# A fused adaLN, attention and mixture-of-experts kernel: the loop over batches written out, and two of eight probability tiles of a head pair normalised by VectorE

## What is computed

```python
h = _layernorm(x, axis=-1) * (1 + ca) + sa
qkv = x @ qkv_w.T                       # x is h here; B, S = 4, 512
scores = jnp.einsum('bhqd,bhkd->bhqk', q, k) * scale + bias
attn = jax.nn.softmax(scores, axis=-1)
a = jnp.einsum('bhqk,bhkd->bhqd', attn, v)
x = x + ga * (a.transpose(0, 2, 1, 3).reshape(B, S, 1024) @ o_w.T)
h = _layernorm(x, axis=-1) * (1 + cb) + sb      # and on to the experts
```

## Time and profile before

| | us |
|---|---|
| median of 3 runs | 1016.47 (1014.36 to 1022.89) |
| the profiled execution, whole time | 1013.81 |
| its span in the profile | 1012.0 |
| PE busy, whole span | 953.2 (94%) |
| DVE busy | 769.4 (76%) |
| ACT busy | 679.4 (67%) |
| POOL busy | 398.1 (39%) |

### The profile page before, as it was taken

How to read it: one execution, slowest core, us unless ns; L and a number is a source line. 1 busy time by engine, 2 the same in 40 slices (tenths; PEclk the granted TensorE clock), 3 DMA queues, 4 the chain that set the end, 5 groups by cost and what they waited for, 6 DMA issues and landing times.

```text
span 1012.0 us, 16804 instructions
## 1 busy us (share of the span) xinstructions
PE 953.2 (94%) x4592; PEld 690.6 (68%) x4592; DVE 769.4 (76%) x1452; ACT 679.4 (67%) x1168; POOL 398.1 (39%) x260
## 2 busy tenths in 40 slices
PE   4889999899998999999969699999999999999997
PEld 2546666566665666666524578888888888888886
DVE  5757667566665666766647589999999999999997
ACT  3556666466665666666626477877777777777775
POOL 0578888688886888888910000000000000000000
PEclk9999999899999999999979899999999999999999
DMA  7885445256444445534200899999999999999991
GB/s 205 258 234 119 97 119 126 63 124 142 113 96 101 96 118 125 125 90 99 66 19 27 204 221 219 223 222 222 223 222 222 221 224 221 223 220 225 220 206 41
DMA packets 71096, 160.39 MB, mean 158 GB/s; under 512 B 10273, under 2 KB 36193, under 8 KB 60945
## 3 DMA queue, kind: packets, MB, share of 16 engines
q1 hardware_dynamic: 71056, 159.97, 70.1%
HBM read 105.60 MB, written 2.42 MB: 107 GB/s over the span
## 4 chain that ended last, share of the span: by engine, by line
PE 84%; DMA 4%; DVE 4%; issue 3%; ACT 2%; SPq 1%; POOL 1%; POOLq 0%; DVEq 0%; ACTq 0%
PE ps L620 40%; PE ps L433 11%; PE ps L420 10%; PE ps L409 5%; PE ps L411 5%; PE ps L383 4%; PE ps L446 3%; PE ps L394 2%; DMA strips<-in_L_ffn_w_down 2%; DMA k_low<-qk 1%; POOL prob L859 1%; DMA comb_rows<-strips 1%; PE ps L538 1%; PE ps L540 0%; DVE qk L959 0%
## 5 line engine op out<-in xcount | busy, mean ns | idle before, releaser
L859 POOL TENSOR_SCALAR prob<-prob,rinv 128x512 f32<-128x512 f32 x256 | 397.9, 1567 | 111.3 <-DVE rinv L993 109.1
L706 ACT ACTIVATE prob<-prob,nmax 128x512 f32<-128x512 f32 x256 | 182.9, 716 | 150.9 <-DVE nmax L976 150.8
L620 PE MATMUL ps<-hT,wT 128*128 128x512 f32 x960 | 244.2, 390 | 0.3 <-DVE wT L1145 0.3
L1164 DVE TENSOR_TENSOR PT<-v_sb,strips 128x1024 f32<-128x1024 f32 x160 | 196.0, 1225 | 41.4 <-ACT v_sb L830 28.3
L830 ACT ACTIVATE v_sb<-ps 128x1024 f32<-128x1024 f32 x160 | 164.5, 1028 | 77.9 <-PE ps L620 77.4
L620 PEld LDWEIGHTS ps<-hT,wT 128*128 128x128 f32 x960 | 180.8, 189 | 39.0 <-ACT strips L805 1.1
L620 PE MATMUL ps<-stack,wT 128*128 128x512 f32 x640 | 198.1, 391 | 9.2 <-DVE wT L1151 9.2
L204 DVE COPY PT<-ps 128x512 f32<-128x512 f32 x128 | 88.4, 691 | 141.2 <-PE ps L420 138.7
L1151 DVE TENSOR_TENSOR wT<-PT,stack 128x1024 fp32r<-128x1024 f32 x160 | 195.0, 1219 | 0.0
L976 DVE CUSTOM_DVE_ANT_0 prob<-ps,strips 128x512 f32<-128x512 f32 x256 | 165.0, 681 | 11.5 <-issue 8.0
L822 ACT CAST stack<-PT 128x1024 fp32r<-128x1024 f32 x160 | 166.6, 1041 | 8.8 <-DVE PT L1164 8.8
(11 more groups left out here) (105 smaller groups left out, 731.1 us busy)
## 6 DMA issues: line engine op xcount, KB each, us to landing
strips<-comb_rows SPq DMA_DIRECT2D x158, 512.0 KB, 10.9
stack<-qk SPq DMA_DIRECT2D x128, 256.0 KB, 3.8
k_low<-qk SPq DMA_DIRECT2D x64, 128.0 KB, 3.9
hT<-qk SPq DMA_DIRECT2D x64, 128.0 KB, 3.8
strips<-bias_rows SPq DMA_DIRECT2D x3, 1792.0 KB, 13.9
strips<-in_L_ffn_w_gate SPq DMA_DIRECT2D x80, 64.0 KB, 9.8
strips<-in_L_ffn_w_down SPq DMA_DIRECT2D x80, 64.0 KB, 11.0
strips<-bias_rows SPq DMA_DIRECT2D x2, 896.0 KB, 5.4
```

The lines of the kernel that those rows point to most:

```text
L620: last = nc.tensor.matmul(ps[:, bank + c, :], weights(a), rows(m, c), start=start and k == 0, stop=stop and k == 2, skip_group_check=True)
L706: nc.scalar.activation(prob[:, u, :], prob[:, u, :], ACT.Exp, bias=nmax[:, u:u + 1], scale=-1.0, accum_out=rsum[:, u:u + 1]).then_inc(s_ex ...
L859: nc.gpsimd.tensor_scalar(prob[:, u, :], prob[:, u, :], rinv[:, u:u + 1], None, ALU.mult).then_inc(s_prob, 1)
L1164: nc.vector.tensor_tensor(weighted[:, k % 4, :], silu[:, k % 2, :], cb[:, r, half * HALF:(half + 1) * HALF], ALU.mult).then_inc(s_mul, 1)
```

## The change

Three things change, all in attention.

First, the loops over batches are written out: `Fori` becomes a Python `for` on PE, ACT, DVE, SP and POOL, and all semaphore targets become constants. Second, of each pair's eight tiles, units 3 and 7 are normalised by DVE, right behind the reciprocal of their two units, and the other six by POOL; a second semaphore, `normalised_by_dve`, counts DVE's. Third, the order of DVE's work within a segment changes: `invert_sums` moves ahead of the copies, and `update_x` and `new_statistics` move from the end of a batch's last pair (n = 9) into the first segment of the next one (n = 2 of the next batch).

```diff
--- before.py
+++ after.py
@@ -165,7 +165,8 @@
         s_s, s_ttr, s_exp, s_t = sem("scores"), sem("biased"), sem("exped"), sem("transposed")
         s_ca, s_cd = sem("copied_by_act"), sem("copied_by_dve")
         s_v, s_vc, s_pv = sem("v_projected"), sem("v_copied"), sem("pv_done")
-        s_rinv, s_prob, s_o = sem("sums_inverted"), sem("normalised"), sem("o_copied")
+        s_rinv, s_o = sem("sums_inverted"), sem("o_copied")
+        s_prob, s_prob_dve = sem("normalised_by_pool"), sem("normalised_by_dve")
         s_ymm, s_yg, s_ytr, s_x2 = sem("y_added"), sem("y_gated"), sem("y_transposed"), sem("x_updated")
 
 
@@ -196,6 +197,12 @@
         def copied(b, g):
 
             return (s_ca if g % 2 == 0 else s_cd), b * (G // 2) + (g // 2 + 1)
+
+        def normalised(b, g):
+
+            if g % 4 == 3:
+                return s_prob_dve, b * (G // 4) + g // 4 + 1
+            return s_prob, b * (G // 4 * 3) + (g // 4 * 3 + g % 4 + 1)
 
         def copy_unit(copy, n, u):
 
@@ -289,7 +296,7 @@
             sp.dma_start(wdsT[:, :], down_shared_t).then_inc(ld["small"], 16)
             sp.dma_start(ebias[:, 0:1], expert_bias[0:P, :]).then_inc(ld["small"], 16)
             sp.dma_start(ebias[0:E - P, 1:2], expert_bias[P:E, :]).then_inc(ld["small"], 16)
-            with sp.Fori(0, B - 1) as b:
+            for b in range(B - 1):
                 for n in range(2, HPAIRS + 2):
                     if n == HPAIRS - 2:
                         sp.wait_ge(s_v, b * HPAIRS + HPAIRS)
@@ -413,7 +420,7 @@
 
             def transpose_probs(b, n, u):
                 g = UNITS * n + u
-                pe.wait_ge(s_prob, b * G + (g + 1))
+                pe.wait_ge(*normalised(b, g))
                 if g >= 2:
                     pe.wait_ge(*copied(b, g - 2))
                 for kb in range(QT):
@@ -506,7 +513,7 @@
             pair(0, 1)
             pe.wait_ge(w_split, 6)
             pe.wait_ge(ld["ow"], 16)
-            with pe.Fori(0, B - 1) as b:
+            for b in range(B - 1):
                 for n in range(2, HPAIRS + 2):
                     pair(b, n)
             for n in range(2, HPAIRS):
@@ -758,7 +765,7 @@
             first_high(1)
             pair(0, 0)
             pair(0, 1)
-            with act.Fori(0, B - 1) as b:
+            for b in range(B - 1):
                 for n in range(2, HPAIRS + 2):
                     pair(b, n)
             for n in range(2, HPAIRS):
@@ -855,14 +862,14 @@
 
                 if u % 2 == 0:
                     pool.wait_ge(s_rinv, b * (G // 2) + (UNITS * n + u) // 2 + 1)
-                    pool.sem_inc(apart, 1)
                 nc.gpsimd.tensor_scalar(prob[:, u, :], prob[:, u, :], rinv[:, u:u + 1], None,
                                         ALU.mult).then_inc(s_prob, 1)
 
-            with pool.Fori(0, B) as b:
+            for b in range(B):
                 for n in range(HPAIRS):
                     for u in range(UNITS):
-                        normalise(b, n, u)
+                        if u % 4 != 3:
+                            normalise(b, n, u)
 
 
         @block.vector
@@ -988,9 +995,14 @@
 
                 g = UNITS * n + u
                 dve.wait_ge(s_exp, b * G + (g + 2))
-                if n >= 1:
-                    dve.wait_ge(s_prob, b * G + (g - UNITS + 2))
+                if n >= 1 or b >= 1:
+                    dve.wait_ge(*normalised(b, g - UNITS))
+                    dve.wait_ge(*normalised(b, g - UNITS + 1))
                 nc.vector.reciprocal(rinv[:, u:u + 2], rsum[:, u:u + 2]).then_inc(s_rinv, 1)
+                if u % 4 == 2:
+                    dve.wait_ge(s_rinv, b * (G // 2) + g // 2 + 1)
+                    nc.vector.tensor_scalar(prob[:, u + 1, :], prob[:, u + 1, :], rinv[:, u + 1:u + 2], None,
+                                            ALU.mult).then_inc(s_prob_dve, 1)
 
             def copy_o(b, n):
                 dve.wait_ge(s_pv, b * HPAIRS + (n + 1))
@@ -1025,20 +1037,23 @@
                 if n == 0:
                     first_low(1)
                     qk_low(b, 1)
+                if n == 2 and b >= 1:
+                    update_x(b - 1)
+                    new_statistics(b - 1)
+                invert_sums(b, n, 0)
                 if n >= 2:
                     copy_o(b, n - 2)
                 if n >= 1:
                     copy_probs(b, n - 1, 5)
-                invert_sums(b, n, 0)
 
                 add_bias(b, n, 2)
                 add_bias(b, n, 3)
                 if n == 0:
                     modulate(2)
                     modulate(3)
+                invert_sums(b, n, 2)
                 if n >= 1:
                     copy_probs(b, n - 1, 7)
-                invert_sums(b, n, 2)
 
                 add_bias(b, n, 4)
                 add_bias(b, n, 5)
@@ -1048,21 +1063,18 @@
                     qkv_low(3)
                     qkv_low(4)
                     qkv_low(5)
+                invert_sums(b, n, 4)
                 copy_probs(b, n, 1)
-                invert_sums(b, n, 4)
 
                 add_bias(b, n, 6)
                 add_bias(b, n, 7)
                 if n == 0:
                     first_low(2)
                     first_low(3)
+                invert_sums(b, n, 6)
                 copy_probs(b, n, 3)
-                invert_sums(b, n, 6)
                 if not (final and n >= HPAIRS - 2):
                     qk_low(b, n + 2)
-                if n == HPAIRS + 1:
-                    update_x(b)
-                    new_statistics(b)
 
             qk_low(0, 0)
             then(statistics(3))
@@ -1074,7 +1086,7 @@
             pair(0, 0)
             pair(0, 1)
             sign_gates()
-            with dve.Fori(0, B - 1) as b:
+            for b in range(B - 1):
                 for n in range(2, HPAIRS + 2):
                     pair(b, n)
             for n in range(2, HPAIRS):
```

## The result

The changed kernel takes a median of 1037.82 us (1036.28 to 1038.24), beside 1015.41 us (1014.2 to 1022.89) for the kernel before on the same chip: a ratio of 1.0222, 95% interval 1.0194 to 1.025. It is slower by 22.4 us. The profiled execution's span is 1034.5 us instead of 1012.0.

What follows compares the result with a forecast made beforehand. PE bounds an ordinary pair at 14.17 us; the new order makes it a 15.67 us ring of waits. +25.4, +3.9, -1.0 and +1.0 give +29.3 on 1013.8, 1043; forecast 1044 us as median, range 1026 to 1066.

Steps and rivals of the forecast that it cites:

- the side that it gave 0.88: Whole kernel: slower than before, against 0.05 for within about 1% and 0.07 for faster by over 1%.
- the ring of waits: Ordinary attention pair: DVE, ACT and PE wait for each other from one copy of unit 7 to the next, 15.67 us.
- Its own bounds, -16 and +20: Scaling 0.22 us instead of 0.50 gives -16; scaling 0.67 and 0.12 more behind each exposed wait give +20.
- The exposed wait: Each segment on DVE: first add to reciprocal takes at least 2.28 us, about 1.06 of it idle waiting for ACT's exponentials.
- The scaling: DVE's scaling of one 512-column tile, units 3 and 7: taken as 0.50 us, 0.69 with the reciprocal ahead of it.
- Up to some 16: Borders of batches: writing the loops out alone gains up to some 16 us of the 17.4 that three borders cost.
- +0.75: Moved x update and statistics on DVE: outlast the wait for exponentials by 0.75 us at each of three borders.
- The ends: Outside pairs 3 to 30: last pairs +3.9 us, end -1.0 at POOL, beginning +1.0 for two scalings.
- That PE stays the bound: Rival for attention: shorter exponential waits keep the ring under 14.17 us, leaving the borders' gain, 998 us; chance 0.07.
- That only DVE's own work counts: Rival for attention pairs: DVE's 14.81 us bounds, PE's part not in series, about 1016 to 1020 us; chance 0.05.
- That DVE and POOL shut each other out: Rival for tile scalings: DVE waits for POOL's tile, 1.7 us later twice a pair, about 1140 us; chance 0.10.
- The clock: Way to be wrong, on PE: its many short waits might lower its clock; no size or chance given.

## Why the prediction was right

It said 1044 us with a range of 1026 to 1066, and 1037.82 was measured, on the side that it gave 0.88. It was right for its own reason: the ring of waits is there, link by link, and the sum was 7 us too high (1043 for the profiled execution, which took 1036.28). Its own bounds, -16 and +20, give 1028 to 1064; the range was 2 us wider on each side without a reason given.

**The ring.** Predicted 15.67 us a pair, measured 15.50. From the rows of the kernel after, in the prediction's order: copy of unit 7 to `attend` 0.79 (0.82 predicted), to the copy of unit 1 3.00 (3.00), to the add 0.65 (0.61), to the reciprocal 2.28 (2.28), reciprocal and scaling 0.60 (0.69), copy 0.60 (0.61), `qk_low` 1.13 (1.12), 2.28 (2.28), 0.09 (0.07), two copies 1.20 (1.22), 2.28 (2.28), 0.60 (0.69). They sum to 15.50. The exposed wait, which was read from one row in pair 1, held to the hundredth, in every segment where it binds. The four runs that put one segment back show which links count, as the prediction had them: segments 0 and 1 do, segment 2 doesn't; 3 does, though its old place is worse. PE's idle time ahead of `attend` was to be 1.2 to 1.6 us and is 1.19, just below.

**The scaling.** This is the term that was mis-sized. 0.50 was taken between bounds of 0.22 and 0.67; DVE passes from scaling to copy in 0.40 (227.00 to 227.40, the instruction 0.49 long), and reciprocal and scaling take 0.60, not 0.69. Twice a pair that is 0.18, the whole difference of the ring, and over 27 pairs 4.9 us of the 5.3 by which pair 3 to pair 30 came out lower. The Trainium skill (VectorE: DVE Perf Modes, "Mode 2×_2P — use both read ports for one tensor") has the two columns a cycle from which I had estimated 0.4 and a forecast 6 us lower; the trace's 0.40 agrees with it.

**The loops.** "Up to some 16" was said to be the borders' gain. Alone it is 12.9: of the 17.4 us over ordinary pairs, 3 x 1.04 remain for `update_x` and the statistics, and 3 x 0.44 for the y transposes, PE's own work, as long as PE is the bound.

**`update_x`.** +0.75 was predicted at each of three borders. DVE at the first border of the kernel after (L1031 is `update_x`, L1023 the statistics):

```profile
171.63 0.17 DVE L1001 RECIPROCAL rinv<-rsum 128x2 f32<-128x2 f32 x1 [0.98 <-ACT prob L713]
...
187.13 0.17 DVE L1001 RECIPROCAL rinv<-rsum 128x2 f32<-128x2 f32 x1 [0.98 <-ACT prob L713]
...
189.57 0.68 DVE L983 CUSTOM_DVE_ANT_0 prob<-ps,strips 128x512 f32<-128x512 f32 x1
...
190.78 0.68 DVE L1031 TENSOR_TENSOR x_all<-x_all,ps 128x512 f32<-128x512 f32 x1
191.50 0.88 DVE L1023 BATCH_NORM_STATS2 stats<-x_all 128x6 f32<-128x128 f32 x4
192.29 0.15 DVE L1001 RECIPROCAL rinv<-rsum 128x2 f32<-128x2 f32 x1
...
203.14 0.17 DVE L1001 RECIPROCAL rinv<-rsum 128x2 f32<-128x2 f32 x1 [0.98 <-ACT prob L713]
```

The reciprocals of segment 3 stand once round the ring from each other. Over the batch's last pair that is 187.13 - 171.63 = 15.50: the y transposes and `gate_y` cost nothing up to there, since PE and DVE have room for them beside the ring. Over the next one it is 203.14 - 187.13 = 16.01, 0.51 more. Of it 0.44 is `update_x` with the statistics: from first add to reciprocal 2.72 instead of 2.28. The rest is about the 0.1 by which the copy of unit 3 comes later behind the reciprocal at 187.13 (at 187.83, 0.70 instead of 0.60): it waits for transposes that end at 187.79 and that the y transposes had put off. The step named the right thing and took it too large, with the 0.17 and 1.00 of the kernel before, and its rows give 0.72 rather than 0.75: now the update and its wait pass in 0.72 instead of 0.78 and the four statistics in 0.79 instead of 1.00. 3 x 0.5 over 27 x 15.50 = 418.5 is 420.0, the way from pair 3 to pair 30.

**The ends.** The last pairs cost 3.5 (3.9 predicted) and the end -1.2 (-1.0). At the beginning +1.0 was taken, for the scalings ahead of the first `qk_low`, and the sum shows -0.3. More than all of that -0.3 lies ahead of the first pair: the first score of pair 0 starts at 28.83 instead of 29.41, and over the thirteen kernels of this case, which do the same work up to there, it starts anywhere from 28.07 to 29.41. From pair 0 to pair 3 it is 49.78 instead of 49.52, so 0.3 for the +1.0; with 48.9 to 50.8 in the other kernels no run tells this from the spread. The experts' part is as long as before within 0.4.

**The rivals.** That PE stays the bound falls by the 2.28 in every pair and PE's 1.19 ahead of `attend`. That only DVE's own work counts falls by the 15.50, over its 14.81, and by the 0.75 us for which DVE waits for PE's transposes ahead of the copy of unit 1 (231.19). That DVE and POOL shut each other out falls by the kernel after, where DVE's scaling goes first and takes 0.49, and, for the case with POOL first, by the run with the scalings one step later. The clock, named as a way to be wrong, stayed up.

## What to carry to other kernels

On an engine that works strictly in order, put an instruction that waits for another engine's result behind everything that is ready, not ahead of it: here one reciprocal of 0.17 us, moved ahead of two copies, made 1.09 us a pair on a kernel whose busy shares hardly changed. This holds for work that is ready: behind the copy of unit 3, which wasn't, the reciprocal stood 0.25 us worse. Look at where each engine's idle time lies rather than at how much there is, and go once round the ring of waits with durations from single rows; such a sum was right to 0.17 us in 15.5. Test the parts of a change with and without each other, since a gain (loops written out: 12.9 us, and 29.4 with the new order and the update's new place) or a cost (two scalings, 0.08 or 0.72 us a pair) depends on what bounds the stage at the time.

## What the runs showed of the hardware

DVE's float32 scaling of 128 x 512 from SBUF to SBUF takes 0.486 us (median of 64) and lets the next instruction start after 0.40. It runs beside GpSimd's own scaling: where DVE starts first by about 0.06 us, GpSimd's tile takes 1.85 us instead of 1.56; where GpSimd is first by 0.4 or 0.6 us, its tile keeps its 1.56 and DVE's scaling is 0.48 to 0.55 long. With GpSimd first by 0.09 or by 1.05 us it was 0.87 and 0.79 long, three times each.

Semaphore targets in registers, which cost nothing in the kernel before, made each wait for ACT 0.17 us longer once DVE was waiting when the signal came.

A hardware loop's return stopped DVE for 3.87 us and, behind DVE, PE for 4.50, and the stop is gone when the loop is written out. The Trainium skill says (Runtime: NRT & Kernel Launch, "Instruction fetch mechanics") that a taken branch to a page outside the prefetched ones stops the engine until that page is fetched; the 3.87 with "issue" as the releaser fit this. In all four such stops of the traces (two before, two in the run with the loops kept) one 8 KB packet of the DMA queue for instructions starts 1.5 to 1.6 us behind DVE's branch, 184.02 behind 182.50 at the first, which fits as well. Whose instructions it carries no view says, so this stays argued.

PE's stops of 1.2 us, one in each pair, left its granted clock at 1.00 in the windows shown; the stop of 4.50 had been followed by 0.52.
